# Four half-and-half expert slots at places 16, 20, 24, 28 instead of 18, 22, 26, 30, and one pair of copies ahead of the last activation

## What is computed

```
scores = softmax(xf @ gate_w.T); _, idx = top_k(scores + gate_b, 2)
w  = take_along_axis(scores, idx)                  # two experts of eight per token
h  = silu((x @ w1[e] + b1[e]) * (x @ w3[e] + b3[e]))   # 256 -> 352, for each expert e
oe = h @ w2[e] + b2[e]
y  = sum over the token's two experts of w * oe
z  = the same form with one shared expert, for every token
out = x + y + z
```

## Time and profile before

| | |
|---|---|
| median of 3 executions | 586.93 us (584.76 to 587.72) |
| the profiled execution | 586.75 us, its span 584.8 us |
| TensorE clock granted, mean | 0.990 |
| PE busy | 563.0 us, 96% |
| DVE, ACT, POOL busy | 442.1, 325.1, 232.3 us |
| the adds (L1762) | 40, from 425.9 us on |

### The profile page before, as it was taken

How to read it: one execution, slowest core, us unless ns; L and a number is a source line. 1 busy time by engine, 2 the same in 40 slices (tenths; PEclk the granted TensorE clock), 3 DMA queues, 4 the chain that set the end, 5 groups by cost and what they waited for, 6 DMA issues and landing times.

```text
span 584.8 us, 11124 instructions
## 1 busy us (share of the span) xinstructions
PE 563.0 (96%) x3656; PEld 426.4 (73%) x3656; DVE 442.1 (76%) x839; ACT 325.1 (56%) x1004; POOL 232.3 (40%) x228
## 2 busy tenths in 40 slices
PE   8999999999999999999999999999999999999980
PEld 6547566788797978789788887887777777667660
DVE  4999999999795979949688689867677556656650
ACT  3632424379869796895967939615223344555220
POOL 1010110307581834387243762635245343444443
PEclk9999999999999999999999999999999999999995
DMA  8920004162741321423215217892644434244323
GB/s 303 348 96 2 1 1 173 44 217 97 265 172 46 122 97 71 147 72 120 99 47 207 71 47 227 274 377 73 171 119 83 72 56 68 43 68 62 54 27 35
DMA packets 36183, 68.37 MB, mean 117 GB/s; under 512 B 5504, under 2 KB 29024, under 8 KB 33632
## 3 DMA queue, kind: packets, MB, share of 16 engines
q1 hardware_dynamic: 28208, 57.99, 29.7%
q0 software_dynamic: 6784, 8.95, 9.2%
q10 hardware_dynamic: 1136, 0.73, 0.4%
HBM read 56.62 MB, written 15.25 MB: 123 GB/s over the span
## 4 chain that ended last, share of the span: by engine, by line
PE 60%; DVE 17%; DMA 9%; issue 7%; POOL 3%; ACT 2%; POOLq 1%; SPq 0%; DVEq 0%
PE pb L743 9%; DMA out_dram<-R 6%; PE pb L635 6%; DVE R L1138 6%; PE pb L498 6%; PE pb L600 6%; PE pb L548 6%; PE pb L564 5%; PE pb L777 5%; PE pb L515 4%; PE pb L647 4%; DVE R L1161 3%; PE pb L612 2%; DMA out_dram<-R,hidx 2%; PE pb L568 2%
## 5 line engine op out<-in xcount | busy, mean ns | idle before, releaser
L895 ACT ACTIVATE R<-R,mx 128x154 f32<-128x154 f32 x256 | 104.4, 415 | 0.1
L1762 POOL DMA_INDIRECT out_dram<-R x36 | 55.6, 1546 | 83.0 <-DMA out_dram<-R 51.1
L743 PE MATMUL pb<-R 128*128 x256 | 81.0, 459 | 0.0
L1020 ACT ACTIVATE R<-R 128x352 f32<-128x352 f32 x36 | 17.9, 497 | 90.5 <-DVE R L1573 76.9
L743 PEld LDWEIGHTS pb<-R 128*128 128x128 f32 x256 | 46.2, 190 | 20.4
L498 PE MATMUL pb<-xnT,wq 128*128 128x256 f32 x256 | 58.2, 383 | 0.0
L886 ACT ACTIVATE R<-pb,bq 128x256 f32<-128x256 f32 x64 | 30.1, 473 | 48.0 <-PE pb L498 47.8
L498 PEld LDWEIGHTS pb<-xnT,wq 128*128 128x128 f32 x256 | 47.7, 190 | 7.8 <-issue 1.2
L907 ACT COPY R<-pb 128x512 f32<-128x512 f32 x80 | 40.8, 616 | 18.4 <-PE pb L548 18.3
L1686 POOL DMA_INDIRECT xs_dram<-xn,pos x32 | 31.9, 996 | 47.2 <-DVE pos L1322 38.9
L895 ACT ACTIVATION_READ_ACCUMULATOR R<-R,mx 128x1 f32 x256 | 49.4, 193 | 0.0
(11 more groups left out here) (203 smaller groups left out, 1179.4 us busy)
## 6 DMA issues: line engine op xcount, KB each, us to landing
R<-in_fside_dram SPq DMA_DIRECT2D x16, 1232.0 KB, 5.6
R<-in_L_ffn_w_dram SPq DMA_DIRECT2D x16, 352.0 KB
R<-in_mask_dram SPq DMA_DIRECT2D x16, 308.0 KB, 2.9
R<-xs_dram SPq DMA_DIRECT2D x32, 129.0 KB, 2.1
KV<-in_ebias_dram SPq DMA_DIRECT2D x2, 1440.0 KB
out_dram<-x SPq DMA_DIRECT2D x4, 512.0 KB, 4.3
R<-in_L_ffn_w_dram SPq DMA_DIRECT2D x8, 256.0 KB, 4.4
x<-in_x_dram SPq DMA_DIRECT2D x3, 512.0 KB, 10.9
```

The source lines that it names most:

```text
L743: ins = e.matmul(pb[:, u.i, 0:F], xsT[:, s % 2, k, :], ew13[:, bass.ds(w_reg[s] * 1408 + q * 704 + k * F, F)], start=(k == 0), stop=(k == 1))
L895: ins = e.activation(att[t % 3][:, h, :], att[t % 3][:, h, :], ACT.Exp, bias=mx[:, a4, 1, h:h + 1], accum_out=mx[:, a4, 2, h:h + 1])
L1762: e.indirect_dma_start(out=out, out_offset=bass.IndirectOffsetOnAxis(ap=to.bitcast(U32), axis=0), in_=rows, in_offset=None, compute_op=ALU ...
```

## The change

The numbers in `MIXED` fall by two, so there are 16 places ahead of the first mixed slot instead of 18, and 7 behind the last instead of 5. The wait for the base rows of the last quarter (`base_out3`) goes to whichever comes first of the mixed slots and slot f = 16. At the last place ACT copies the transposed hidden rows of place 34 ahead of the SiLU of place 35, instead of behind it.

```
-MIXED = (18, 22, 26, 30)
+MIXED = (16, 20, 24, 28)
...
+                if s == NS - 1:
+                    hidden_turned(s - 1)
                 if s < NS:
                     silu(s)
-                if s >= 1:
+                if s >= 1 and s != NS - 1:
                     hidden_turned(s - 1)
...
-                if s == FULL[NA]:
+                if s == min(FULL[NA], MIXED[0]):
                     w.wait_ge(base_out3, 16)
```

## The result

The changed kernel takes 588.91 us (median of 11, 586.98 to 590.53) against 585.94 us before (median of 11, 584.76 to 587.72). The ratio estimated from all the runs is 1.0041, 95% interval 1.0028 to 1.0054: slower by 2.4 us, between 1.6 and 3.2. The medians alone lie 3.0 us apart (0.51%). 588.91 is inside the band that I had called no difference (584.0 to 589.9), and the forecast was 589.2 us. The profiled execution took 589.09 us, its span is 587.2 us.

A forecast was written before the change was run, and what follows sets the result against it. POOL's queue of adds was taken to set the end. Its steps from place 15 on summed to 89.77 us against 87.57, begun 0.29 later: 586.75 + 2.49 = 589.24, forecast 589.2 us, range 586.0 to 591.0.

The forecast's parts named there:

- The bound: POOL's queue of adds sets the end; the chain leaves PE near 490 us instead of 514.
- The kinds of the twelve steps between full slots: Add queue from place 15 on: six expert changes at 4.61 us, five same-expert steps at 1.87, one at 2.72.
- The steps into mixed slots: Add of a full slot to that of the next mixed slot: four at 5.19, 20.76 us against 20.13 before.
- my condition: Steps into mixed slots cost 5.11, 5.10, 5.35 us where the full slot ahead had itself waited, 4.57 otherwise.
- The halves: Adds of mixed slots: 3.39 us between halves, 3.93 to the next slot, together 7.32, four times 29.28.
- The start: Add of place 15 comes 0.29 us later, at 489.79, half of the mixed slot's 0.58 on PE.
- The end: Last add on POOL starts at 579.56 us, 2.49 us later than before.
- the price list: Add-to-add distances on POOL by kind: mixed slot 7.32 us, step into one 5.19, expert change 4.61, same expert 1.87.
- Hidden things: Place 35's result 1 to 2 us late, weight copies, base-row wait, ACT's copies before the last SiLU: all worth nothing.
- keep up: Rival: adds follow the results, the last add starts at 571.31, 5.8 us sooner; 581.0 us in all; chance 0.08.
- Rival 2: Adds behind adds that had waited land late; the sum rises by 2.1 us to 591.3; chance 0.27.
- Rival 3: Landings vary, so no net difference: 587.8 us, or 587.5 with the shift of 0.29 covered; chance 0.20.

The follow-up runs named there:

- e2: The kernel before with only ACT's copies moved ahead of the last SiLU; 585.55 us, ratio 0.9997.
- e1: The changed kernel with ACT's copies at the last place left as before, mixed slots at 16, 20, 24, 28; 588.72 us against 585.64, ratio 1.0059.
- e8: The changed kernel with mixed slots at 12, 16, 20, 24 and SP's reads to match; 582.56 us, ratio 0.9956 to before.
- e4: The changed kernel with mixed slots at 15, 19, 23, 27 and SP's reads to match; 584.45 us, ratio 0.9979 to before.
- e9: The kernel before with mixed slots at 12, 16, 20, 24, reads to match, base-row wait as in the changed kernel; 582.43 us, ratio 0.9948.
- e10: e8 once more, measured beside e9; 582.51 us, ratio 0.9960 to before.

## Why the prediction was right

- **The bound.** Right. The add queue sets the end, and from place 15 on, as said (PE leaves the chain at 489.3, forecast near 490).
- **The kinds of the twelve steps between full slots.** Right for all twelve. Changes: 4.45, 4.57, 4.84, 4.58, 4.58, 4.57, together 27.59 us (sum: 27.66). Same expert: 2.02, 1.87, 1.88, 1.86, 1.86, together 9.49 (9.35), and 2.67 (2.72). The four steps hidden before did turn out as changes.
- **The steps into mixed slots.** This term was mis-sized: 4.63, 4.55, 4.55, 4.65, together 18.38 us against 20.76 in the sum. I had read 5.11, 5.10 and 5.35 as the price behind an add that had itself waited. In e2, with the slots where they were before, the same steps took 4.68, 4.61, 4.56 and 4.61 (the first two ended at VectorE's result), in e1 4.46 (likewise), 4.70, 4.41 and 4.51. A step into a mixed slot costs about what any waited step costs, 4.6. The high figures of before were late landings: its chain has 4.32 us for the add of place 21 and 4.58 for that of place 29, where 3.7 to 3.9 is usual (the add of place 17 is not in the chain). Nor did my condition fit all three: the adds of places 17 and 21 had waited for a result, not for a landing, by my own list.

```profile
516.14 4.32 DMA out_dram<-R
...
553.37 4.58 DMA out_dram<-R
```

- **The halves.** 30.82 us against 29.28: one first half landed after 4.75 us instead of 3.1 (550.47 to 555.49). This late landing, on the other side, hid part of the error above. The queue from place 15 on took 88.95 us against 89.77.
- **The start.** The add of place 15 came at 490.51 instead of 489.79. Of the 1.01 us against before, 0.57 was there at the first result of the stage (425.19 against 424.62), which is a difference of executions, ahead of the change's reach. The 0.44 that is left (0.32 in e1) is near the 0.29 of the forecast.
- **The end.** 579.46 against 579.56: closer than its terms deserve. Three errors (-2.4, +1.5, +0.7) cancel. That the place of the last add came out to 0.1 us is luck. The loss itself was right in size without it: 2.4 us by the ratio, 3.0 by the medians, where I had 2.5. With the measured 4.6 for steps into mixed slots on both sides the price list gives 1.6 + 0.3 = 1.9 us, which lies in the interval (1.6 to 3.2); whether anything beyond the list is in the loss is not shown. The profiles of e1 and e2, each the shorter one of its placement (151.9 and 150.9), differ by 1.0 us only. Late landings, which count where the queue sets the end, could make the rest of the measured loss; that was not tested.
- **Hidden things.** The result of place 35 was late for its buffer, as forecast (3.31 us of idle time), and cost nothing; copies of weights, reads and the wait for the base rows cost nothing that shows (no add from mixed slot 16 on waits for VectorE's result or for SP); the second part cost and gave nothing (e2).
- **The rivals.** The queue does not keep up in the changed kernel; it nearly does in e8, whose last add starts 1.4 us behind the last result. Rival 2 fell: the time is 588.91 where it had 591.3, and in the profile after, the four steps behind adds that had waited (19, 23, 27 and 30) all took 4.55 to 4.65. Late landings exist, but not there for that reason. Rival 3 had 0.6 to 0.9 us of difference (587.5 to 587.8); the interval of the result begins at 1.6.

## What to carry to other kernels

Where a queue of ordered transfers sets the end, write down the distance from each to the next and sort the distances by what they wait for; the change is then a sum over kinds, and which data meet in which step can be counted from the inputs. By the placements measured here, put a step that must wait anyway (here a mixed slot) where two steps would wait anyway, and early, so that cheap steps are left at the end to catch up in: 12, 16, 20, 24 is 0.4% faster than before, though 16, 20, 24, 28 is 0.4% slower. This tuning depends on how many tokens each expert gets: with other inputs the steps of the same expert fall elsewhere, by the way the slots are filled; no run here had other inputs.

## What the runs showed of the hardware

An accumulating indirect transfer of 128 rows of 1 KB is waited for in a step of 4.4 to 4.8 us as a rule, start to start, and one of 64 rows in 3.3 to 4.0. Now and then one lands 0.5 to 1.6 us late: 4.75 us for 64 rows in the changed kernel, where 3.0 to 3.3 is usual, a step of 5.45 in e4. Most of the late ones met other places in other profiles. The four first halves in the profile of e1, with the same placement as the changed kernel, had none:

```profile
549.39 1.43 POOL L1762 DMA_INDIRECT out_dram<-R  x1 [2.96 <-DMA out_dram<-R]
552.73 1.43 POOL L1762 DMA_INDIRECT out_dram<-R,hidx  x1 [1.91 <-DMA out_dram<-R]
```

3.34 us there, 5.02 in the changed kernel's profile. e1's profiled execution, 586.21 us, was the fastest of its six, the slowest took 590.59; with the slots at 12 the executions lie within 582.28 to 583.27 in the first series, 582.44 to 584.31 in the second. One long step came back, though: the one from place 15 into mixed slot 16 with the slots at 12 took 5.13, 5.38 and 5.29 us in e8, e9 and e10, so not every long step is chance. Late landings, which count only where the queue sets the end, would fit as the source of the spread, but that was not tested: what makes a landing late stays open.
